# Two re-sequenced attentions, another begin of the head loop, and unread products at five waits

## The reference, cut to what matters

```
x = conv0(x);  x = x + conv1(gn(x));  t = tokens(x)           # t: [4, 1024, 128]
t = t + attn2(ln(t))       # 4 heads of 32, causal
t = t + ffn2(ln(t))        # top half of the tokens by a router weight, 128 -> 512 -> 128
t = t + attn3(ln(t))       # 16 heads of 64, three branches, mixed by gates:
                           #   o1: causal over all keys, o2: over 256 selected keys,
                           #   o3: causal in a window of 64
t = t + ffn3(ln(t))        # 8 experts, one each token, 640 places an expert
```

## Time and profile before

| what | value |
|---|---|
| runs | 2813.05, 2812.11, 2804.85 us; median 2812.11 |
| profiled execution | 2809.78 us, of which the profile's span is 2805.0 |
| PE / PE weight loads busy | 2438.3 us (87%) / 1668.8 us (59%) |
| DVE / ACT / POOL busy | 1888.1 (67%) / 1468.1 (52%) / 1305.7 (47%) |
| mean granted PE clock | 0.92 of 2.4 GHz |
| conv / attn2 / ffn2 | 0 to 191 / 191 to 446 / 446 to 568 us |
| latents / heads' preamble | 568 to 701 / 701 to 767.5 us |
| head loop, 16 passes | 767.5 to 2619.5 us |
| ffn3 | 2619.5 to 2805 us |

### The profile page before, as it was taken

The page is one execution under the profiler, slowest core; times in us unless marked ns, Lnnn a source line. Parts: engine busy times, 40 slices in busy tenths (PEclk is TensorE's granted clock), DMA queues, the critical chain, the costliest instruction groups (busy, mean ns, idle before and its releaser), DMA issues. The chain is left out here.

```text
span 2805.0 us, 51467 instructions
## 1 busy us (share of the span) xinstructions
PE 2438.3 (87%) x16517; PEld 1668.8 (59%) x16517; DVE 1888.1 (67%) x3715; ACT 1468.1 (52%) x2524; POOL 1305.7 (47%) x884
## 2 busy tenths in 40 slices
PE   5398896855699999999999998999999999999757
PEld 3166663544466666666666665666665666666646
DVE  2767763667486776867767667676675766867526
...
DMA packets 85091, 131.82 MB, mean 47 GB/s; under 512 B 16224, under 2 KB 60768, under 8 KB 84624
## 3 DMA queue, kind: packets, MB, share of 16 engines
...
...
## 5 line engine op out<-in xcount | busy, mean ns | idle before, releaser
L2448 ACT ACTIVATE a_PT<-PS 128x512 f32<-128x512 f32 (+1 forms) x1111 | 617.2, 586 | 411.7 <-PE PS L2320 313.4
L2178 POOL TENSOR_TENSOR a_KT<-a_PT 128x512 f32<-128x512 f32 (+2 forms) x179 | 418.8, 2355 | 600.9 <-ACT a_PT L2448 600.0
L2178 POOL TENSOR_TENSOR a_KT<-a_KT,a_PT 128x2048 f32<-128x2048 f32 (+3 forms) x128 | 391.4, 3058 | 7.5
L2517 DVE TENSOR_REDUCE a_NM<-PS 128x2 fp32r<-128x512 f32 x460 | 292.1, 685 | 102.1 <-PE PS L2270 96.6
L2319 PE MATMUL PS<-a_QH,a_K 128*128 128x512 f32 (+3 forms) x768 | 313.9, 415 | 0.0
L2319 PE MATMUL PS<-a_QH,a_KSW 128*128 128x256 f32 (+2 forms) x848 | 309.8, 385 | 0.0
L2531 DVE TENSOR_REDUCE a_MX<-PS 128x1 f32<-128x512 f32 (+3 forms) x432 | 264.4, 665 | 39.1 <-PE PS L2284 24.9
L2320 PE MATMUL PS<-a_QL,a_K1B 76*128 76x512 f32 (+3 forms) x768 | 262.1, 348 | 0.0
L2281 PE MATMUL PS<-a_K,a_QH 128*128 128x512 f32 (+3 forms) x768 | 245.6, 392 | 0.3
L2267 PE MATMUL PS<-a_KSW,a_QH 128*128 128x512 f32 x460 | 197.7, 482 | 0.8
L2483 DVE TENSOR_TENSOR a_R<-PS,a_angles 128x512 f32<-128x512 f32 x153 | 102.4, 687 | 128.9 <-ACT a_TM L2399 128.4
...
## 6 DMA issues: line engine op xcount, KB each, us to landing
...
slots<-in_empty_slots SPq DMA_DIRECT2D x1, 5160.0 KB, 20.0
...
c_EX<-in_experts SPq DMA_DIRECT2D x1, 4608.0 KB, 18.0
```

The costliest lines, as they stand in the source:

```text
L2178: nc.gpsimd.tensor_tensor(total, one_in, other_in, ALU.add).then_inc(s["added"], 1)
L2448: nc.scalar.activation(PT[:, to:to + width], turning(key)[:, 0:width], ACT.Exp).then_inc(s["taken"], 1)
L2517: ins = nc.vector.tensor_reduce(out, bank.rearrange("p (a n) -> p a n", a=2), AX.X, ALU.max, negate=True)
```

## The change

1. ORDER2 is replaced by another permutation of the same 576 words.
2. ORDER is replaced by another permutation of the same 283 words, with the same "+" marks.
3. The head loop's begin: SP loads angles, then the seven loads of load.next in another order (XS, WKS first), and WP only behind the preamble's steps, with a semaphore of its own (projection) that PE waits for before the loop. POOL issues its three transfers once the seven loads have landed. PE waits for them only at score.0.0 of the preamble. PE makes 60 unread bf16 products of 128x384 before its first wait, and two before each a, tr, v and near of the preamble (35 steps).
4. A helper, hold_clock, makes unread fp32 products of 128x128 into P[7]: 60 in stage_conv behind the logits, 30 in stage_ffn2 and 45 in stage_latents ahead of the first transposes, and in stage_ffn3 45 ahead of the first transposes and 90 ahead of turn_tokens(0).

Of the two strings only the parts of which the text speaks are shown:

```diff
@@ -303,6 +303,7 @@
 
+                hold_clock(nc, P[7], ident, 60)
...
@@ -475,47 +476,47 @@
 ORDER2 = """
-tx.1.0 st.2 tx.1.1 v.1.0 rep.0.0 qk.1.0.0 qk.1.0.1 v.1.1 rep.0.1 far.0.0.0 far.0.1.0 far.0.1.1 far.0.2.0 sd.2
...
-far.0.7.4 score.0.9.1 value.0.6 far.0.7.5 far.0.7.6 far.0.7.7 join.0.6 score.0.10.0 join.0.7 qk.1.1.1 norm.0.1 score.0.10.1 score.0.11.0 turn.0.3
-value.0.7 value.0.8 value.0.9 add.0.6 value.0.10 add.0.7 add.0.8 xn.2 score.0.12.0 score.0.12.1 score.0.13.0 score.0.13.1 rep.1.1 score.0.14.0
-project.0.1 st.3 value.0.11 score.0.14.1 score.0.15.0 score.0.15.1 tx.2.0 score.0.16.0 score.0.16.1 tx.2.1 value.0.12 value.0.13 value.0.14 add.0.9
-sum.0.2 add.0.10 value.0.15 norm.0.2 score.0.17.0 score.0.17.1 score.0.18.0 far.1.0.0 far.1.1.0 far.1.1.1 value.0.16 sd.3 score.0.18.1 add.0.11
...
-far.1.7.4 far.1.7.5 far.1.7.6 far.1.7.7 add.1.5 score.1.8.0 rep.2.1 score.1.8.1 score.1.9.0 far.2.0.0 far.2.1.0 join.1.7 score.1.9.1 score.1.10.0
...
-score.1.16.0 score.1.16.1 add.1.11 add.1.12 add.1.13 far.2.4.2 far.2.4.3 far.2.4.4 value.1.14 value.1.15 xn.3 score.1.17.0 score.1.17.1 score.1.18.0
...
-far.2.5.3 far.2.5.4 far.2.5.5 score.2.0.1 score.2.1.0 add.1.15 add.1.16 add.2.0 add.2.1 tx.3.0 value.2.0 far.2.6.0 tx.3.1 score.2.2.0
...
+xn.1 tx.1.0 tx.1.1 st.2 v.1.0 qk.1.0.0 qk.1.0.1 rep.0.1 qk.1.1.0 qk.1.1.1 far.0.0.0 far.0.1.0 far.0.1.1 far.0.2.0
...
+rep.1.0 add.0.1 turn.0.1 score.0.2.0 xn.2 score.0.2.1 score.0.3.0 far.0.4.1 far.0.4.2 score.0.3.1 score.0.4.0 score.0.4.1 score.0.5.0 st.3
...
+far.1.0.0 score.0.10.1 score.0.11.0 far.1.1.0 value.0.7 value.0.8 value.0.9 join.0.6 join.0.7 far.1.1.1 project.0.1 turn.0.3 add.0.7 add.0.8
...
+value.1.0 join.1.6 value.1.1 sum.0.3 norm.0.3 add.1.1 sum.1.0 tx.2.0 tx.2.1 far.1.7.5 score.1.6.0 score.1.6.1 far.1.7.6 far.1.7.7
...
+add.1.4 value.1.2 value.1.3 add.1.5 value.1.4 rep.2.0 value.1.5 project.1.0 score.1.8.0 score.1.8.1 xn.3 sum.1.1 norm.1.1 score.1.9.0
+score.1.9.1 score.1.10.0 value.1.6 value.1.7 score.1.10.1 add.1.6 add.1.7 add.1.8 rep.2.1 tx.3.0 tx.3.1 score.1.11.0 score.1.12.0 score.1.12.1
+value.1.8 project.1.1 qk.3.0.0 qk.3.0.1 far.2.0.0 qk.3.1.0 qk.3.1.1 add.1.9 value.1.9 score.1.13.0 far.2.1.0 far.2.1.1 far.2.2.0 score.1.13.1
...
@@ -1006,6 +1007,12 @@
+def hold_clock(nc, bank, ident, times):
+    for _ in range(times):
+        nc.tensor.matmul(bank[:, 0:128], ident[:, :], ident[:, :], start=True, stop=True)
...
@@ -1053,6 +1060,7 @@
+                hold_clock(nc, P[7], ident, 30)
                 scores(0)
...
@@ -1309,6 +1317,7 @@
                 pe.wait_ge(s["ld"], 96)
                 pe.wait_ge(s["one"], 1)
+                hold_clock(nc, P[7], ident, 45)
@@ -1317,6 +1326,7 @@
                 pe.wait_ge(s["slot_ready"], B)
+                hold_clock(nc, P[7], ident, 90)
                 turn_tokens(0)
...
@@ -1822,76 +1833,76 @@
 ORDER = """
-wk tr.q2 split.tr.q2 tr.q3 split.tr.q3
+wk tr.q2 tr.q3 split.tr.q2 split.tr.q3
 score.4.0
-score.4.1 v.v1.0 v.v1.1
+score.4.1 v.v1.0 near.4.0
 score.4.2
-score.4.3 near.4.0 near.4.1
-score.5.0 near.4.2 near.4.3 near.5.0 value.4.4 near.5.1 near.5.2 near.5.3
-score.5.1 near.6.0
+score.4.3
+score.5.0 +load.next near.4.1 near.4.2 near.4.3
+score.5.1 near.5.0
 score.5.2
-score.5.3 near.6.1 near.6.2 near.6.3 turn.0.2 near.7.0 value.5.5 near.7.1 near.7.2 k1.0 near.7.3
-score.6.0 split.k1.0 add.4
-score.6.1 +load.next turn.0.3 sum.1 norm.1 value.6.6 k1.1
-score.7.0 k1.2 split.k1.1 split.k1.2 k1.3 split.k1.3
+score.5.3 near.5.1 near.5.2 v.v1.1 near.5.3 near.6.0 value.4.4 near.6.1 near.6.2 near.6.3 turn.0.2 near.7.0 value.5.5 add.4 near.7.1 near.7.2 k1.0 near.7.3
+score.6.0 split.k1.0 k1.1 sum.1 norm.1 turn.0.3 k1.2 split.k1.1 split.k1.2
+score.6.1 k1.3 split.k1.3
+score.7.0
 score.7.1
-score.8.0
...
+score.22.0
+score.22.1
 score.22.2
-score.22.3 +near.2.0 +near.2.1 +near.2.2
-score.23.0 +turn.0.0 +near.2.3 +near.3.0 +near.3.1
-score.23.1
-score.24.0 value.21.21 value.22.22 add.17 +near.3.2 +near.3.3 add.18
-+score.0.0
-+score.0.1 +turn.0.1 +tr.w3 value.23.23 add.19 +double.s value.24.24 add.20 sum.5 +rope.q2 norm.5
-+score.1.0 project.4
+score.22.3 +near.2.0 +near.2.1
+score.23.0 +near.2.2 +near.2.3
+score.23.1 +double.w2 +near.3.0 add.17 +near.3.1 +turn.0.0
+score.24.0 +near.3.2 +near.3.3 +a.w3 +a.q2 +rot.q2
++score.0.0 +turn.0.1 value.22.22 add.18 value.23.23 value.24.24 add.19 +rot.w3 add.20 sum.5 norm.5
++score.0.1
++score.1.0
 +score.1.1
-+score.2.0 ysum.5 +split.tr.w3
++score.2.0
 +score.2.1
-+score.3.0 project.5 +v.vw.0 +v.vw.1 +v.vs.0 +double.w3 +a.q3 +value.0.0 +value.1.1 +value.2.2 +add.0 +add.1 +double.w2 +value.3.3 +add.2 +add.3 +sum.0 +rot.q3 +rope.q3 +norm.0
++score.3.0 +rope.w3 +v.vw.1 +rope.q2 ysum.5 +v.vs.0 +tr.w3 +split.tr.w3 +a.q3 +rot.q3 +double.w3 project.5 +value.0.0 +value.1.1 +value.2.2 +add.0 +add.1 +value.3.3 +add.2 +add.3 +sum.0 +rope.q3 +norm.0
 """
...
@@ -2062,7 +2073,7 @@
-        s = {n: keep.enter_context(nc.semaphore("a3_" + n)) for n in (*plan.sem, "ready", "ld", "rows")}
+        s = {n: keep.enter_context(nc.semaphore("a3_" + n)) for n in (*plan.sem, "ready", "ld", "projection", "rows")}
...
@@ -2102,10 +2113,9 @@
                         if q is not None:
                             after(sp, q, at, ("filled", plan.jobs[-1][0]))
                             sp.wait_ge(s["ready"], 7)
-                        for dst, src in ((XC[:, :], entry[:, 0:N]), (XS[:, :], entry[:, 3 * N:3 * N + KEEP3]),
+                        for dst, src in ((XS[:, :], entry[:, 3 * N:3 * N + KEEP3]), (WKS[:, :], d["wks"][bass.ds(g * C, C), :]),
+                                         (XC[:, :], entry[:, 0:N]), (WKW[:, :], d["wkw"][bass.ds(g * C, C), :]),
                                          (WQ[CKW:, :], d["wq3"][bass.ds(g * QR_, QR_), :]),
-                                         (WKW[:, :], d["wkw"][bass.ds(g * C, C), :]),
-                                         (WKS[:, :], d["wks"][bass.ds(g * C, C), :]),
                                          (WVW[:, :], d["wvw"][bass.ds(g * C, C), :]),
                                          (WVS[:, :], d["wvs"][bass.ds(g * C, C), :])):
...
@@ -2140,9 +2150,9 @@
-                for dst, src in ((angles[:, :, :, :], d["angles"]), (WP[:, :, :], d["w_proj3"])):
-                    sp.dma_start(dst, src).then_inc(s["ld"], 16)
+                sp.dma_start(angles[:, :, :, :], d["angles"]).then_inc(s["ld"], 16)
                 one_pass(0, 0, None)
+                sp.dma_start(WP[:, :, :], d["w_proj3"]).then_inc(s["projection"], 16)
...
@@ -2199,9 +2209,9 @@
-                pool.wait_ge(s["ready"], 7)
-                for x, t in enumerate(upper):
-                    pool.dma_start(t[DH:DH + ROWS, :, :], d["branch_rows"][:, x, :, 0:t.shape[2]]).then_inc(s["rows"], 16)
+                pool.wait_ge(s["ld_next"], 16 * 7)
+                for x in (2, 1, 0):
+                    pool.dma_start(upper[x][DH:DH + ROWS, :, :], d["branch_rows"][:, x, :, 0:upper[x].shape[2]]).then_inc(s["rows"], 16)
                 one_pass(None)
...
@@ -2354,11 +2364,18 @@
+                def keep_clock(count):
+                    for _ in range(count):
+                        nc.tensor.matmul(P[7][:, 0:384], identb[:, :], masks.rearrange("p a n -> p (a n)"), start=True, stop=True)
                 def one_pass(g, q):
+                        if q is None and what in ("a", "tr", "v", "near"):
+                            keep_clock(2)
...
@@ -2374,6 +2391,8 @@
+                            if q is None and key == ("score", 0, 0):
+                                pe.wait_ge(s["rows"], 48)
                             key_major(key, q, at)
...
@@ -2382,10 +2401,10 @@
+                keep_clock(60)
-                pe.wait_ge(s["rows"], 48)
-                pe.wait_ge(s["ld"], 32)
                 one_pass(None, None)
+                pe.wait_ge(s["projection"], 16)
...
@@ -2586,7 +2605,7 @@
-                dve.wait_ge(s["ld"], 32)
+                dve.wait_ge(s["ld"], 16)
```

More of the change, by code:

```diff
@@ new lines @@
+far.0.4.3 value.0.0 rep.1.1 value.0.1 sum.0.0 far.0.4.4 far.0.5.0 far.0.5.1 value.0.2 far.0.5.2 far.0.5.3 far.0.5.4 far.0.5.5 value.0.3
+join.0.4 join.0.5 sd.3 v.1.1 norm.0.0 add.0.2 far.0.6.0 far.0.6.1 far.0.6.2 turn.0.2 score.0.6.0 far.0.6.3 value.0.4 value.0.5
+far.0.6.4 score.0.6.1 score.0.7.0 add.0.3 add.0.4 project.0.0 far.0.6.5 far.0.6.6 far.0.6.7 far.0.7.0 score.0.7.1 value.0.6 far.0.7.1 far.0.7.2
+far.0.7.3 sum.0.1 far.0.7.4 score.0.8.0 score.0.8.1 score.0.9.0 far.0.7.5 far.0.7.6 far.0.7.7 norm.0.1 score.0.9.1 score.0.10.0 add.0.5 add.0.6
@@ L519 @@
+score.3.18.0 add.3.13 score.3.18.1 score.3.19.0 add.3.14 add.3.15 add.3.16 value.3.16 norm.3.2 value.3.17 value.3.18 value.3.19 sum.3.3 norm.3.3
 project.3.2 project.3.3
@@ L1861 @@
 score.17.0
 score.17.1
-score.17.2 +a.q0
-score.17.3
-score.18.0 +rope.w1 +tr.w1 double.k1 sum.4 +rot.q0 +rope.q0
-score.18.1
-score.18.2 norm.4
-score.18.3 +tr.q0 value.17.17 value.18.18 +split.tr.w1 add.14 +split.tr.q0 +a.w2 +a.q1
-score.19.0 ysum.4 +rot.w2
```

(21 more changed lines are left out.)

101 lines of the change are left out of this document (49 added, 52 removed).

## The result

The changed kernel takes 2760.64 us (median of four runs, 2755.48 to 2771.17) against 2808.48 for the kernel before in the same comparison. The ratio is 0.9836 with a 95% interval of 0.9805 to 0.9866: 46 us less, between 38 and 55. The forecast was 2793 with a range of 2757 to 2826, so the range held it near its lower end, and the forecast's own 2778 to 2803 did not. The profiled execution is the fastest of the four, 2755.48 us with a span of 2751.5.

The account below looks back on a forecast made before the run. The head loop was taken as bound by PE's own work, so an order wins only waits. Terms −8 −10 −0.5 +1.5 +5 +1 −1.5 −6 = −18.5 us gave 2791.3 profiled, 2793 median; range 2757 to 2826.

Parts of the forecast that it names:

- rival 4: Clock stays up in the second attention (−25 us) and the loop loses its start wait (−32): 2754.6 us; chance 0.15.
- (a): Head loop, each pass: a.w3 and a.q2 put between near.3.3 and score.0.0 cover the 1.03 us wait: −1.1 us.
- (b): Head loop, pass start: near.4.0 replaces v.v1.1, the 1.61 us wait stays, score.4.3 follows closer on ScalarE: +0.3 us.
- (c): Head loop, each pass: k1.0 to k1.3, sum.1 and norm.1 ahead of far.0 to far.3 load DVE together: +0.4 us.
- an order can win only PE's waits: Head loop: it is PE's own work, so reordering saves only waits; −8 us over 16 passes.
- the 10 us set against them: Second attention: costs of the new order set against its gains: +2.2, +5 and +2.8 us.
- DVE's excess of 5: Second attention, far.0.0.0 to far.1.0.0: DVE has 31.8 us of maxima and splits beside 26.7 of PE: +5 us.
- the 2.8 for short waits: Second attention: a few short waits in an order packed anew: +2.8 us.
- The second forty products: Second attention: qk.1.1.0 and qk.1.1.1 now stand ahead of the second forty unread products and far.0.0.0: +2.2 us.
- Rival 3: Unread fp32 products only delay; 3.2, 3.5 and 4.7 us are not given back by the clock: 2805 us; chance 0.07.
- WP's wait: Heads' begin: WP issued behind the last doubling and tr.w3 ending the preamble make PE wait: +2 us.
- Rival 1: Head loop: k1 products wait for DVE's reductions, 1.5 us net a pass, +24 for −8: 2825.6 us; chance 0.20.

## Why the prediction was right, and where it was not

The direction and the range were right. The likeliest sum was 18.5 us where 46 came. By the prediction's own sign it was wrong all the same: a loop period that moves by over 1 us was to refute it whatever the other stages did, and it moved by 2.6. That the time lies in the range is owed to the range's width: its lower end was drawn for rival 4, whose mechanism in the loop did not occur. That part is luck.

**Head loop: -8 forecast, 38 to 40 measured.** The waits came as they were put: (a) gone, (b) still there with 0.53 added where I had 0.3, (c) nothing where I had 0.4. Idle time over 0.15 us went from 3.42 to 2.96 us a pass, the 0.46 of the forecast. The step that failed is the one in front of them, "an order can win only PE's waits". In the two profiles the 38.5 us of fifteen passes are

- 7 us of waits (15 x 0.46), as forecast;
- 18 us of PE's busy time in the steady pass, 1.2 a pass at full clock. Some 0.7 of it are transposes and the masks' products, of which PE has as many as before and gets to the next one sooner;
- 13 us of irregular passes: 18.0 us over fifteen steady passes before, 5.0 after. The two reloads are 11.8 of the 18.0 (120.5 + 119.9 - 2 x 114.3), and the rest are low starts. That 115.5 was over 114.3 stood in the earlier trace rows against the passes' own lengths, and I took it as given.

What (a) is worth depends on its surroundings. Its own length was right: 1.1 us forecast, 1.2 by the steady pass (113.8 against 112.6). Undone alone in the changed kernel it costs 33.6 us of loop, 15.6 of them for passes with a low start. That is no share of the 38.5: the kernel with (a) undone has eleven low starts where the one before had seven. In the old sequence, covering the same wait gave 17 us of loop, of which 6 are the steady pass. In the attention I had added the clock behind a wait; in the loop I had not, although the mean there was 0.99 and not 1.00.

**Second attention: -10 forecast, -20 measured.** The waits went as forecast, 11 us against 14 gross, with 3.11 at tx.3.0 where I had 3. The clock gave 9 where I had 6. What failed is the 10 us set against them: DVE's excess of 5 between far.0.0.0 and far.1.0.0 shows as waits of 1.55 and 1.11 us for the turned maxima and shorter ones, and the 2.8 for short waits did not come. The second forty products do start late, 3.4 us later in the stage, 1.3 of it by the longer wait at tx.1.0 (3.20 for 1.91). The tail's wait grew from 3.35 to 5.89. A static count of two engines' work in a stretch overpriced the excess here. And the 20 us belong to the shorter of the stage's two lengths: in three of the eight profiles of this sequence the stage takes 248 us, and the gain is 13.

**Unread fp32 products: +5.5 forecast, +6 measured alone.** Their lengths, delays and parts given back (2 and 4.7 us in the second FFN and the latents) came near the sum. Rival 3 did not happen in full: the clock behind them was higher in all three places, but in the third, at 0.64, by little. The rule of the Trainium skill (TensorE: Matmul & The Clock Gate, Part 4: PE-mode transpose) that transposes do not count as busy PE in the way of other products is neither needed nor refuted by this. In the third FFN it agrees with the trace in that the clock fell to half 6 us into the transposes and narrow products, at 2584 us.

**Third FFN: +1 forecast for its front, +9.5 in the profile.** 4.8 of it is the delay as worked out (5.7 in the sum). Two profiles with the 45 products and without the pause told next, the one with the fp32 products alone and the one with (a) undone, have +3.5 and +0.5 for this stretch: there 1.7 and 3.6 us are given back where I had 4.7. The other part of the 9.5 is that pause: the last placement starts on DVE 11 us after PE's last product. Such pauses stand in five of fourteen profiles, with these unread products or not, also in the kernel with xn.2 moved, where the same stretch took 79.7 us instead of 74. They belong to the execution and not to the change, and I don't know their cause.

**Begin: -6 forecast.** The loads gave 5.7 where I had 3.8, the unread bf16 products nothing that the runs can show where I had 4, and WP's wait is 2.54 where I had 2. Its removal left the first pass as long as it was (114.9 for 115.0), so its price was not its length.

**Rivals.** Rival 1 (DVE at k1) did not occur. Rival 4 came closest with 2754.6, with the loop at 38 and the attention at 20, but not by its mechanism: the wait at the pass's start stayed.
